# Eight blocks written out, state work dropped where a batch has no state, and a new order of items on each engine

## The reference

```
xn  = layernorm(x)
out = x + attn(xn) + ffn(xn)

ffn:  silu(xn @ Wg.T) * (xn @ Wu.T) @ Wd.T            # 512 -> 2048 -> 512
attn: h = rmsnorm(xn) * w;  q, k, v = h @ ternary(Wqkv).T    # 16 heads of 32
      for each chunk of 128 tokens, S = 0 at the start of a batch:
          scores = (q k') * mask[h, t, s]              # decays with t - s
          o = scale * (scores v + lam_t * q S)
          S = lam_T * S + (lam_rev * k)' v
      rmsnorm twice, then @ ternary(Wproj).T
```

## Time and profile before

| | |
|---|---|
| median of 3 runs | 1431.11 us |
| the profiled execution's own time | 1432.87 us |
| its span | 1431.2 us |
| TensorE busy | 1362.1 us (95%) |
| VectorE busy | 959.0 us (67%) |
| ScalarE busy | 491.6 us (34%) |
| GpSimd busy | 70.4 us (5%) |

### The profile page before, as it was taken

The page is one execution under the profiler, slowest core; times in us unless marked ns, Lnnn a source line. Parts: engine busy times, 40 slices in busy tenths (PEclk is TensorE's granted clock), DMA queues, the critical chain, the costliest instruction groups (busy, mean ns, idle before and its releaser), DMA issues.

```text
span 1431.2 us, 23359 instructions
## 1 busy us (share of the span) xinstructions
PE 1362.1 (95%) x8412; PEld 730.6 (51%) x8412; DVE 959.0 (67%) x1943; ACT 491.6 (34%) x921; POOL 70.4 (5%) x107
## 2 busy tenths in 40 slices
PE   5788889999999999999999999999999999999998
PEld 2344445555545555455545555455554555445553
DVE  5787777566765667656774667656676666755677
ACT  7755422232322323323322333233232332322332
POOL 5510000000000000000000000000000000000000
PEclk9898989999999999999999999999999999999999
DMA  7223104211251123511153111521225112351215
GB/s 259 117 96 111 52 27 101 81 37 45 60 129 36 30 45 74 130 36 45 30 98 97 30 46 45 112 82 30 45 60 134 34 33 44 79 124 30 45 30 118
DMA packets 202815, 102.19 MB, mean 71 GB/s; under 512 B 135616, under 2 KB 187840, under 8 KB 201024
## 3 DMA queue, kind: packets, MB, share of 16 engines
q1 hardware_dynamic: 202400, 100.45, 28.1%
q10 hardware_dynamic: 288, 0.01, 0.0%
HBM read 35.40 MB, written 8.39 MB: 31 GB/s over the span
## 4 chain that ended last, share of the span: by engine, by line
PE 89%; DVE 4%; DMA 2%; issue 2%; SPq 1%; ACT 1%; POOL 0%; DVEq 0%; ACTq 0%; POOLq 0%
PE bank L515 85%; PE bank L557 2%; PE bank L583 1%; DMA stage<-stage 1%; SPq L919 1%; PE bank L584 1%; DMA k_stack<-k_parts 0%; DVE arena L845 0%; DMA stage<-down_t 0%; DMA q_stack<-q_parts 0%; DVE arena L738 0%; DMA xin<-x 0%; ACT wd_hi L1124 0%; SPq L921 0%; PE bank L615 0%
## 5 line engine op out<-in xcount | busy, mean ns | idle before, releaser
L515 PE MATMUL bank<-wd_hi,arena 128*128 128x512 f16 x1024 | 318.4, 381 | 0.0
L515 PE MATMUL bank<-xt,wu_hi 128*128 128x512 f16 x1024 | 306.8, 381 | 8.6 <-DVE wu_lo L1277 8.2
L515 PE MATMUL bank<-xt,wg_hi 128*128 128x512 f16 x1024 | 308.0, 383 | 2.0 <-DVE xt L739 2.0
L515 PE MATMUL bank<-xt,wg_lo 128*128 128x512 f16 x512 | 195.8, 382 | 0.0
L515 PE MATMUL bank<-xt,wu_lo 128*128 128x512 f16 x512 | 194.9, 381 | 0.0
L515 PE MATMUL bank<-wd_lo,arena 128*128 128x512 f16 x512 | 194.8, 380 | 0.0
L665 ACT ACTIVATE sm_hi<-sm 128x512 f16<-128x512 f32 x128 | 80.4, 628 | 253.9 <-DVE sm L780 253.9
L515 PEld LDWEIGHTS bank<-wd_hi,arena 128*128 128x128 f16 x1024 | 100.5, 98 | 116.0 <-issue 2.3
L515 PEld LDWEIGHTS bank<-xt,wu_hi 128*128 128x128 f16 x1024 | 98.2, 98 | 110.4 <-DVE wu_lo L1277 8.7
L515 PEld LDWEIGHTS bank<-xt,wg_hi 128*128 128x128 f16 x1024 | 98.4, 99 | 104.2 <-issue 3.8
L726 ACT ACTIVATE arena<-sg 128x512 f16<-128x512 f32 x125 | 78.4, 628 | 198.3 <-DVE sg L892 198.1
(11 more groups left out here) (202 smaller groups left out, 1528.1 us busy)
## 6 DMA issues: line engine op xcount, KB each, us to landing
q_stack<-q_parts SPq DMA_DIRECT2D x192, 64.0 KB, 2.2
k_stack<-k_parts SPq DMA_DIRECT2D x192, 64.0 KB, 2.2
xin<-x SPq DMA_DIRECT2D x34, 256.0 KB, 4.5
arena<-x SPq DMA_DIRECT2D x8, 1024.0 KB, 5.6
out<-arena SPq DMA_DIRECT2D x32, 256.0 KB, 2.6
stage<-up_t SPq DMA_DIRECT2D x4, 1024.0 KB, 5.0
stage<-down_t SPq DMA_DIRECT2D x4, 1024.0 KB, 5.4
stage<-gate_t SPq DMA_DIRECT2D x3, 1024.0 KB, 5.5
```

What stands on the lines that cost most here:

```text
L515: last = e.matmul(dst, a, b, start=start and n == 0, stop=stop and n == len(lhs) - 1)
```

## The change

The hardware loop goes: `blocks` now calls the body for blocks 0 to 7 in Python, so each engine has one straight list of instructions and all semaphore values are constants. The clamp of the state, its tables and the semaphore `sp_turn` go. OX with c = 0 and s < 4 is left out in even blocks (`crossed`), and VectorE copies instead of adding to a zero state. The second half of KV (matmuls and update) is left out for s >= 4 in odd blocks (`kept`). The last block leaves out ST, XN, TX, TH and XT. The order of items is new on all engines. SyncE's stores of y are items of their own (YS), the transposes' DMAs wait for the matmuls that still read their targets, and a few further waits are written out.

```diff
     def at(self, blk, k):
-        if isinstance(blk, int):
-            return self.before + self.per * blk + k
-        return blk * self.per + (self.before + k)
+        return self.before + self.per * blk + k
...
 STEADY_ORDER = {
     "PE": [
-        ('V', 0), ('K', 0), ('V', 1), ('G', 0), ('Q', 0), ('U', 0), ('G', 1), ('SC', 0, 0), ('U', 1), ('O', 0, 0),
+        ('K', 0), ('Q', 0), ('U', 0), ('V', 0), ('G', 0), ('V', 1), ('SC', 0, 0), ('G', 1), ('U', 1), ('KV', 0),
...
+NEXT_X = ("ST", "XN", "TX", "TH", "XT")
 def items(blk, engine):
-    return (FIRST_ORDER if isinstance(blk, int) else STEADY_ORDER)[engine]
+    order = (STEADY_ORDER if blk > 0 else FIRST_ORDER)[engine]
+    return [it for it in order if blk < NBLK - 1 or it[0] not in NEXT_X]
+def crossed(blk, s, c):
+    return c == 1 or s >= GROUPS or blk % BPB > 0
+def kept(blk, s):
+    return s < GROUPS or blk % BPB < BPB - 1
...
-            for c in range(2):
+            for c in range(2 if kept(blk, s) else 1):
                 t = slice(P * c, P * (c + 1))
                 last = products(bank[:, t], [kt[0][:, t], kt[0][:, t], kt[1][:, t]],
...
         elif kind == "OX":
+            if not crossed(blk, s, c):
+                return
...
-            e.scalar_tensor_tensor(out=state1[:, :], in0=state[:, a, j, :], scalar=part[:, 4, j:j + 1],
-                                   in1=kvm[:, 0, :], op0=ALU.mult, op1=ALU.add).then_inc(ve["S1"].sem, 1)
+            if crossed(blk, s, 0):
+                e.scalar_tensor_tensor(out=state1[:, :], in0=state[:, a, j, :], scalar=part[:, 4, j:j + 1],
+                                       in1=kvm[:, 0, :], op0=ALU.mult, op1=ALU.add).then_inc(ve["S1"].sem, 1)
+            else:
+                e.tensor_copy(state1[:, :], kvm[:, 0, :]).then_inc(ve["S1"].sem, 1)
...
     def blocks(e, body):
-        body(0)
-        with e.Fori(1, NBLK) as blk:
+        for blk in range(NBLK):
             body(blk)
...
-                        for c in range(2):
+                        for c in range(2 if blk < NBLK - 1 else 0):
                             load_x(e, blk, row, c)
...
                     elif kind == "TH":
+                        for name, uses in (("V", 4), ("Q", 8), ("K", 8)):
+                            e.wait_ge(pe[name].sem, pe[name].at(blk, uses))
                         e.wait_ge(ve["TH"].sem, ve["TH"].at(blk, n + 1))
-                        e.sem_inc(sp_turn, 1)
...
-                    elif it in adds and all(i[-1] != it[-1] for i in adds[adds.index(it) + 1:]):
+                    elif kind == "YS":
...
-                if not isinstance(blk, int):
-                    e.wait_ge(ve["S2"].sem, ve["S2"].at(blk, 0))
-                    e.tensor_scalar(state[:, 0, :, :].rearrange("p j n -> p (j n)"),
-                                    state[:, 0, :, :].rearrange("p j n -> p (j n)"),
-                                    keep[:, 0, bass.ds(blk, 1)], keep[:, 1, bass.ds(blk, 1)], ALU.max, ALU.min)\
-                        .then_inc(ve["KEEP"].sem, 1)
-                    e.wait_ge(ve["KEEP"].sem, ve["KEEP"].at(blk, 0))
```

More of the change, by code:

```diff
@@ L338, in build @@
     cd = table(NQ)
-    keep = table(2, NBLK)
     beta = table(18)
@@ L360, in ahead @@
     def ahead(blk):
-        return isinstance(blk, int) and blk < 0
+        return blk < 0
     C = lambda name, per, before=0: Count(nc, name, per, before)
@@ L450, in z_parts @@
     def z_parts(blk, c):
-        return z_odd if c == 3 or c == 1 and not isinstance(blk, int) else z_even
+        return z_odd if c == 3 or c == 1 and blk > 0 else z_even
     def paired(blk, h):
-        return isinstance(blk, int) and h < TILES_AHEAD
+        return blk <= 0 and h < TILES_AHEAD
     def gate_tile(blk, h):
@@ L483, in shared_free @@
         wrapped = n < N_SHARED
-        if wrapped and isinstance(blk, int):
+        if wrapped and blk <= 0:
             return None
-        other = order[n - N_SHARED]
+        owner = blk - 1 if wrapped else max(blk, 0)
+        other = pooled(owner)[n - N_SHARED]
         kind, k = other[0], other[1] + 1
@@ L495, in shared_free @@
         if kind in ("D", "PJ"):
-            cnt, k = ve["Y"], y_adds(blk).index(other) + 1
+            cnt, k = ve["Y"], y_adds(owner).index(other) + 1
         else:
             cnt = ve[{"ZT": "Z", "KV": "KVM"}.get(kind, kind)]
-        return cnt.sem, cnt.at(0 if ahead(blk) else blk, k - (cnt.per if wrapped else 0))
+        return cnt.sem, cnt.at(owner, k)
     def tensor_item(e, it, blk):
         kind = it[0]
-        if kind in ("KT", "ZT") and not isinstance(blk, int) or kind in ("TX", "TH") and not ahead(blk):
+        if kind in ("KT", "ZT") and blk > 0 or kind in ("TX", "TH") and not ahead(blk):
             return
@@ L583, in tensor_item @@
                 e.matmul(both[:, h, :, :], smp[0][:, h, :], vh, start=h == 0, stop=False)
-                e.matmul(both[:, h, 0, :], smp[1][:, h, :], vh[:, 0, :], start=False, stop=False)
+                alone = h + 1 == HPG and not crossed(blk, s, c)
+                last = e.matmul(both[:, h, 0, :], smp[1][:, h, :], vh[:, 0, :], start=False, stop=alone)
+            if not crossed(blk, s, c):
+                last.then_inc(pe["O"].sem, 1)
         elif kind == "OX":
@@ L648, in scalar_item @@
             e.wait_ge(pe[kind].sem, pe[kind].at(blk, it[1] + 1))
-            if it[1] or not isinstance(blk, int):
+            if it[1] or blk > 0:
                 e.wait_ge(stacked[kind].sem, stacked[kind].at(blk, 48 * it[1]))
-            if kind == "K" and it[1] and isinstance(blk, int):
+            if kind == "K" and it[1] and blk <= 0:
                 e.wait_ge(pe["KV"].sem, pe["KV"].at(blk, it[1]))
@@ L964, in body @@
             def body(blk):
-                row = (blk + 1) % NBLK * BLK
+                row = (blk + 1) * BLK
                 adds = y_adds(blk)
                 for it in items(blk, "SP"):
-                    if it == (("YL", 0) if isinstance(blk, int) else ("V", 0)):
-                        if isinstance(blk, int):
+                    if it == (("YL", 0) if blk <= 0 else ("V", 0)):
+                        if blk <= 0:
                             e.wait_ge(*cut(2))
@@ L1063, in first_item @@
                     last.then_inc(s_arg, 1)
-                    e.memset(state[:, 0, :, :], 0.0)
-                    for m in range(NBLK):
-                        bound = 0.0 if m % BPB == 0 else float(np.finfo(np.float32).max)
-                        e.memset(keep[:, 0, m:m + 1], -bound)
-                        e.memset(keep[:, 1, m:m + 1], bound)
                 elif kind == "RD" and n >= POOL_TERNARY:
@@ L1125, in first_item @@
                 elif kind == "WA":
+                    what = PIECES[n][0]
                     e.wait_ge(ld_piece[slot_of(n)], 16 * sum(slot_of(m) == slot_of(n) for m in range(n + 1)))
+                    if n and PIECES[n - 1][0] == "down" and what != "down":
+                        e.wait_ge(s_red, n)
                     e.activation(squares_to(n), slot(n), ACT.Square, accum_out=pm[:, n:n + 1]).then_inc(s_red, 1)
```

89 lines of the change are left out of this document (47 added, 42 removed), and 217 rows, old and new, of tables (FIRST_ORDER, STEADY_ORDER, ve).

## The result

The changed kernel takes 1362.34 us (median of 4 runs, 1361.45 to 1364.02), the kernel before, run beside it, 1431.96 us (1429.44 to 1433.11): a ratio of 0.9517 [0.9501, 0.9534]. The forecast was 1391 us, with 1372 to 1415 as its range.

The account below looks back on a forecast made before the run. TensorE, busy 1362.1 of 1431.2 us, bounds the kernel. Less 18.1 us (jumps, left-out work, tail) and 22 us (block 0's order), plus 1.7 us outside the span, less 1.8 us for the median: 1391 us, range 1372 to 1415.

Parts of the forecast that it names:

- Block 0, the rest: Block 0 after 85.28 us: units in every gap before scores win idle time and slow clock; 16 of 32 us taken.
- The first rival: Block 0's new order gives nothing, its work standing in another but equal jam: 1413 us, chance 0.20.
- Block 0, the opening: Block 0 up to the first scores: VectorE's new order lets U 4 start 7 us sooner; net gain 6 us.
- The price of the table loads: Block 0 before its first scores: two extra table loads of 1.28 us for the exponentials, and G 6 waits 2 us.
- The later blocks: Seven blocks after block 0 lose 9.3 us of jump waits and 2.8 + 2.7 us of left-out work: 14.8 us.
- Third rival: The 9.3 us at block starts is the bank, not the jump, or straight code stalls elsewhere: 1400 us, chance 0.07.
- The term left at 0: Blocks 1 to 7, score matmul of step 1: the 5.5 us of score waits stay; ends -5.5 and +21 us.
- The second rival: Blocks 1 to 7: chain before step 1's scores keeps 11.0 us, 5.9 us longer each: 1432 or 1454 us, chance 0.10.
- The tail: After TensorE's last matmul: without transposes the store follows the last add, 3.9 us in place of 6.3, saving 2.4 us.

## Why the prediction was right and wrong

**Block 0, the rest: the step that failed.** "I take half, 16 us", because "VectorE limits this". All of the 32 us that the profile offered came, 34.1 in fact: 21.3 of idle time and 12.8 of slow clock, where I had priced the latter at 10. VectorE is now busy 117.4 of 129.5 us there, 91%, and TensorE waits for it once, 0.9 us. A limit by VectorE's busy time alone would have allowed 159.3 - 120.5 = 38.8 us, more than all of the 32; halving them had no row behind it. The two kernels with fewer units ahead of the scores show the mechanism: the gap before SC is what counts. In the first of them the scores that waited started 5.6 to 7.3 us after the last Q or K matmul; a gap filled with less costs idle time and clock. The first rival (nothing from block 0) is refuted by the 40.4 us of its order alone.

This step alone doesn't carry the time out of the range. The prediction says that its range leaves out a block 0 that wins all of its 32 us, but by its own sum that is 1391 - 16 = 1375 us, which lies inside. The rest came from the later blocks (10.3 us) and the opening (2.3).

**Block 0, the opening.** Right in mechanism and nearly in size: 8.3 us against 6; U 4 at 46.55 (48.5), first scores at 71.83 (74). The 2.7 us of slow clock in it had no term. Undoing VectorE's order alone loses 5.2 us. The contention is there too: the halves of WC of piece 3 take 2.06 and 2.02 us beside GpSimd's rounding, and one of these rows is:

```profile
42.98 2.06 DVE L1292 SCALAR_TENSOR_TENSOR wu_lo<-stage,small,wu_hi 128x1024 f16<-128x1024 f32 x1
```

The GpSimd instruction beside it ends at 43.96, and this one 1.08 us later, at 45.04. The same 1.08 us, within 0.02, lies between the two ends for the half before it and for the one behind it. An overlapped WC thus ends as if it had begun its own work when GpSimd's instruction was over.

The price of the table loads was wrong: the wait at G 6 was real, and taking it away gained nothing.

**The later blocks.** The forecast of -14.8 us held in its work (5.5 of the 6.4 to 6.6 us lie here) and roughly in its jumps: 9.3 us of waits, 10.3 from start to start. Third rival: half right. No other stall came with straight code, but the 9.3 us weren't the jump alone. They were the part of a jump of 3.8 to 4.3 us that VectorE's late adds had kept TensorE from hiding. Two things were missed. The term left at 0 was wrong: SC 1 0's 5.5 us went altogether. I had named SyncE's long issue and kept it, but it hung on where an instruction fetch met an issue. Straight code took most of it away (5.0 of 6.6 us from start to start), and ScalarE's order keeps the shorter gap free of it. And the new order gained something that I had at nothing: fewer OX right behind O. Measured from start to start in the two traces, the parts are 5.3 us of work, 10.3 at the jumps, 6.6 at SC 1 0 and 2.7 at the OX that moved, together 24.9 of 25.1 us.

**The second rival** didn't come: SC 1 0 had no wait in the later blocks. Its limit of about 2.5 us was not put to the test there; with ScalarE's order turned back a wait of 2.3 us was not followed by half clock. One end that the prediction gives this term, +21 us, doesn't match the rival's own 41 us (24 without the slow clock); nothing else rests on it.

**The tail.** 3.2 us, not 3.9: the last store's issue ends at 1357.63, and 2.1 us later, not 2.6, the program is done.

## What to carry to other kernels

Before cutting a ceiling in half, ask which row holds it down; here none did, and TensorE's idle time brought a third to six tenths as much again in slow clock. The gap to fill is known from the chain behind it (here 5.6 to 7.3 us from the last Q or K matmul to the scores): count the work in the gap, and fill it up. A stall at a loop's jump is shown only as far as the engine could not run ahead, so look at what held the last instructions before the jump, look for the branch's own row, and don't take an idle row of another engine there as its price. And when an experiment gives the number that was asked for, count whether it moved as many instructions as the change did: 4.6 us came out here for 49 OX, where the change had moved 32.

## What was not expected of the hardware

- The backward jump kept TensorE's sequencer for 3.3 to 4.5 us, and cost TensorE from 0.0 to 2.0 us of it, by when its last banks were freed.
- DMA issues of SyncE took up to 2.00 us instead of 0.60 when a 16 KB packet of instructions was under way, in the loop and in straight code. One of them:

```profile
436.32 1.91 SPq L919 DMA_DIRECT2D k_stack<-k_parts  x1
```

- An f32 matmul pair (OX) holds TensorE 0.22 us behind a matmul of 512 columns and 0.30 behind ones of 32.
- Waits of 1.5 to 2.6 us did not always bring the clock down: 13.2 us idle cost 4 us, 29.1 us cost 13.9.
